# Reordering the hand-written schedule of a two-layer kernel: batch 2's projection between batch 0's pooled blocks, and four smaller moves

## The reference

```python
x = x + moe(lora(x, language_of_batch))          # layer 0
x = x + bit_ffn(attention_pool(x, kind_of_batch)) # layer 1
```

## Time and profile before

| | before |
|---|---|
| median of 3 runs | 734.63 us (733.26 to 735.54) |
| profiled execution: its time | 732.48 us |
| profiled execution: span from the first to the last instruction | 730.6 us |
| busy PE, DVE, ACT, POOL | 687.2, 474.9, 483.9, 390.2 us |

### The profile page before, as it was taken

How to read it: one execution, slowest core, us unless ns; L and a number is a source line. 1 busy time by engine, 2 the same in 40 slices (tenths; PEclk the granted TensorE clock), 3 DMA queues, 4 the chain that set the end, 5 groups by cost and what they waited for, 6 DMA issues and landing times.

```text
span 730.6 us, 9852 instructions
## 1 busy us (share of the span) xinstructions
PE 687.2 (94%) x3238; PEld 421.8 (58%) x3238; DVE 474.9 (65%) x866; ACT 483.9 (66%) x725; POOL 390.2 (53%) x427
## 2 busy tenths in 40 slices
PE   9899989999999999998788899999999999898997
PEld 6333667777777777783455455655556555453443
DVE  4288554545445545540356797887978879897895
ACT  1245436666367778871454979698796978968783
POOL 0202614563442615314867677777777767755554
PEclk9999999999999999999999999999999999999999
DMA  6999889998483948629302021131220111212122
GB/s 221 293 400 352 260 316 364 316 326 311 122 230 130 211 150 208 165 27 251 135 1 87 1 85 52 51 117 48 98 59 29 59 58 31 72 45 71 57 74 73
DMA packets 42627, 108.81 MB, mean 149 GB/s; under 512 B 5424, under 2 KB 7232, under 8 KB 39504
## 3 DMA queue, kind: packets, MB, share of 16 engines
q1 hardware_dynamic: 34352, 94.50, 36.7%
q0 software_dynamic: 7424, 13.06, 9.9%
q10 hardware_dynamic: 800, 0.61, 0.3%
HBM read 88.42 MB, written 28.13 MB: 160 GB/s over the span
## 4 chain that ended last, share of the span: by engine, by line
PE 48%; POOL 13%; issue 12%; ACT 7%; DVE 6%; DMA 3%; POOLq 0%; DVEq 0%; ACTq 0%; SPq 0%
PE ps L979 7%; PE ps L981 7%; PE ps L980 7%; PE ps L1416 6%; PE ps L1386 6%; PE ps L186 5%; POOL ht L1333 2%; POOL x_l L1237 2%; PE ps L971 2%; PE ps L970 2%; ACT h L1647 1%; ACT h L1640 1%; POOL xb L1341 1%; DMA choices<-token_choices,row_of_slot 1%; PE ps L1444 1%
## 5 line engine op out<-in xcount | busy, mean ns | idle before, releaser
L1386 PE MATMUL ps<-ff_q,qt 128*128 128x512 bf16 x512 | 124.2, 386 | 4.9 <-POOL qt L1295 3.3
L1416 PE MATMUL ps<-ff_q,ht 128*128 128x512 bf16 x512 | 120.8, 380 | 0.6 <-DVE res L1835 0.3
L797 POOL DMA_INDIRECT x_after_experts<-y,row_of_slot x32 | 51.6, 1612 | 130.0 <-DVE y L918 100.3
L979 PE MATMUL ps<-w_h,inner_l 128*128 128x512 f32 x256 | 102.0, 398 | 5.4 <-DVE inner_l L930 5.4
L1822 DVE SCALAR_TENSOR_TENSOR h<-ps,scale,bias 128x1024 f32<-128x1024 f32 x64 | 81.9, 1279 | 28.3 <-PE ps L1386 26.0
L981 PE MATMUL ps<-w_h,inner_h 128*128 128x512 f32 x256 | 100.1, 391 | 0.0
L980 PE MATMUL ps<-w_l,inner_h 128*128 128x512 f32 x256 | 100.0, 390 | 0.0
L865 ACT ACTIVATE inner_h<-ps 128x512 fp32r<-128x512 f32 x64 | 37.9, 592 | 70.5 <-PE ps L971 70.4
L1386 PEld LDWEIGHTS ps<-ff_q,qt 128*128 128x128 bf16 x512 | 48.0, 99 | 63.4 <-issue 8.2
L1827 DVE TENSOR_REDUCE h_mx<-h 128x1 f32<-128x1024 f32 x64 | 77.4, 1210 | 10.4 <-ACT h L1640 10.2
L1416 PEld LDWEIGHTS ps<-ff_q,ht 128*128 128x128 bf16 x512 | 48.8, 98 | 54.7 <-issue 1.8
(11 more groups left out here) (262 smaller groups left out, 1342.3 us busy)
## 6 DMA issues: line engine op xcount, KB each, us to landing
w_in_sb<-in_w_in_t SPq DMA_DIRECT2D x8, 2048.0 KB, 15.6
w_raw<-in_w_out_t SPq DMA_DIRECT2D x16, 1024.0 KB, 7.1
x_after_experts<-in_x SPq DMA_DIRECT2D x8, 1024.0 KB, 12.9
x_sum<-in_ff_t SPq DMA_DIRECT2D x8, 1024.0 KB, 9.8
raw<-in_ff_t SPq DMA_DIRECT2D x8, 1024.0 KB, 7.3
x<-x_after_experts SPq DMA_DIRECT2D x32, 256.0 KB, 2.9
out<-res SPq DMA_DIRECT2D x32, 256.0 KB, 3.1
x_sum<-x_after_experts SPq DMA_DIRECT2D x7, 1024.0 KB, 5.5
```

What stands on the lines that cost most here:

```text
L979: pe.matmul(ps[:, s, :], inner_l[:, r, c], w_h[:, k % RING, :], start=k == 0, stop=False)
L1386: m = pe.matmul(ps[:, ff_bank(t, half) + n, :], qt[:, t // TPB % 2, t % TPB, k, :], ff1_q[:, k, f * 512:(f + 1) * 512], start=k == 0, stop ...
L1416: mm = pe.matmul(ps[:, out_bank(t), :], ht[:, t % 2, k // 2, k % 2, :], ff2_q[:, k, :], start=k == 0, stop=k == KF - 1)
```

## The change

The edits, by block:

- Opening: `warm_up` counts 8, 2, 4 become 10, 4, 0. `expand(1, 1)` comes whole before `find(1, 0)`, where its last two products came after `find(1, 1)`.
- Last expert: `inner_block(e, 7)` comes ahead of `out_part(e, 5, 0)`, and the parts of s = 0 ahead of others.
- POOL: batch 1's two `x_low` come after `prob_low(0)` and after `exp_args(1)`; `x_high(2)` after `prob_low(1)`; `exp_args(2)` ahead of batch 2's `x_low`.
- PE: batch 2's `project` and `turn_x` lie between batch 0's pooled blocks; `turn_q(0)` ahead of `pool_block(1, 0)`. Other banks take batch 1's sums and batch 2's keys, and waits move with them.
- ACT: batch 0's squares in two pairs around `keep_x(2, 2..3)`, after `exps(1)`; `keep_sums(1)` before `attend(2)`.
- DVE: `norms(0)` before `greatest(0)`; `keep_q(0)` before `maxima(2)`.
- Loop, steps 22 and 26 (not full): `quantise` in two pieces, `turn_q` a step later, DVE's `keep_q` later.

```diff
-                    warm_up(pe, 8, FIND_BANK)
+                    warm_up(pe, 10, FIND_BANK)
...
-                    warm_up(pe, 2, FIND_BANK)
+                    warm_up(pe, 4, FIND_BANK)
...
-                    warm_up(pe, 4, FIND_BANK)
...
-                    expand(1, 1, range(0, 2))
+                    expand(1, 1)
                     find(1, 0)
                     find(1, 1)
-                    expand(1, 1, range(2, KD))
...
+                        inner_block(e, 7)
                         pe.wait_ge(in_l, KI * e + 6)
                         pe.wait_ge(w_l_cp, KI * e + 6)
                         out_part(e, 5, 0)
                         out_part(e, 5, 1)
-                        inner_block(e, 7)
-                        out_part(e, 5, 2)
                         pe.wait_ge(in_l, KI * e + 7)
                         pe.wait_ge(w_l_cp, KI * e + 7)
                         out_part(e, 6, 0)
-                        out_part(e, 6, 1)
                         pe.wait_ge(in_l, KI * e + 8)
                         pe.wait_ge(w_l_cp, KI * e + 8)
                         out_part(e, 7, 0)
+                        out_part(e, 6, 1)
                         out_part(e, 7, 1)
-                        out_part(e, 6, 2)
-                        out_part(e, 7, 2)
-                        for k in (5, 6, 7):
-                            out_part(e, k, 3)
+                        for s in (2, 3):
+                            for k in (5, 6, 7):
+                                out_part(e, k, s)
...
-            key_bank = lambda b: 0 if b == 1 else SMALL
+            key_bank = lambda b: {1: 0, 2: TRA}.get(b, SMALL)
...
-            num_bank = lambda b, j: (NUM, 0, 1, OUT)[j] if b < 2 else (NUM, NUM, ATT_BANK, NUM)[j]
+            num_bank = lambda b, j: ((NUM, 0, 1, OUT), (0, 1, NUM, OUT))[b][j] if b < 2 else (NUM, NUM, ATT_BANK, NUM)[j]
...
-                    for b in (0, 1):
-                        x_high(b)
-                        x_low(b, 0)
-                        x_low(b, 1)
+                    x_high(0)
+                    x_low(0, 0)
+                    x_low(0, 1)
+                    x_high(1)
...
                     exp_args(0)
                     split_side_keys(0)
                     prob_low(0)
+                    x_low(1, 0)
                     exp_args(1)
-                    x_high(2)
+                    x_low(1, 1)
                     split_side_keys(1)
                     gains(0)
                     prob_low(1)
+                    x_high(2)
+                    unpack_q(0)
+                    exp_args(2)
                     x_low(2, 0)
-                    unpack_q(0)
                     x_low(2, 1)
-                    exp_args(2)
...
-                            pe.wait_ge(pool_cp, 2 * TPB - 1)
+                            pe.wait_ge(pool_cp, TPB + 2)
...
+                        if b == 3 and k == 1:
+                            pe.wait_ge(key_cp, 3)
...
-                        elif b >= 2:
+                        elif b >= 3:
                             pe.wait_ge(sum_l_cp, 2 * b)
...
-                        if j == (1 if b >= 2 else 0) and b + 1 < BATCH:
+                        if j == 1 and b != 1 and b + 1 < BATCH:
                             pe.wait_ge(key_cp, b + 2)
...
-                    for j in range(TPB):
-                        pool_block(0, j)
+                    pool_block(0, 0)
+                    pool_block(0, 1)
                     project(2, 0)
                     project(2, 1)
                     turn_x(2, 2, -1)
                     turn_x(2, 3, -1)
+                    pool_block(0, 2)
+                    pool_block(0, 3)
+                    side_sums(1)
                     project(2, 2)
                     project(2, 3)
-                    side_sums(1)
                     score(2)
-                    pool_block(1, 0)
                     turn_q(0)
-                    for j in range(1, TPB):
+                    for j in range(TPB):
                         pool_block(1, j)
...
-                        if j == 2 and inside(bq, BATCH):
+                        if j == 2 and inside(bq, BATCH) and full(i):
                             turn_q(bq)
                         if j == 3 and inside(bp, BATCH):
                             pool_block(bp, 2)
+                        if j == 3 and inside(bq, BATCH) and not full(i):
+                            turn_q(bq)
...
-                    for j in range(TPB):
-                        square(0, j)
                     exps(1)
+                    square(0, 0)
+                    square(0, 1)
                     keep_x(2, 2)
                     keep_x(2, 3)
+                    square(0, 2)
+                    square(0, 3)
                     prob_high(1)
+                    keep_sums(1)
                     attend(2)
-                    keep_sums(1)
...
                         if inside(t0, TILES):
                             gelu_half(t0, 0)
+                        if j == 2 and inside(bq, BATCH) and not full(i):
+                            quantise(bq, range(0, 2))
...
+                        if j == 2 and inside(bq, BATCH) and not full(i):
+                            quantise(bq, range(2, TPB))
...
+                    norms(0)
                     greatest(0)
-                    norms(0)
                     sums_low(1)
                     keep_keys(2)
+                    keep_q(0)
                     maxima(2)
-                    keep_pool(1, 0)
-                    keep_q(0)
-                    for j in range(1, TPB - 1):
+                    for j in range(TPB - 1):
                         keep_pool(1, j)
...
-                            if j == 3 and inside(bq, BATCH):
-                                keep_q(bq)
                             if inside(t3 - 1, TILES) and not full(i - 1):
                                 finish(t3 - 1)
                             if inside(t0, TILES):
                                 add_bias(t0, 0)
                             if inside(t2, TILES):
                                 keep_h(t2)
+                            if j == 3 and inside(bq, BATCH):
+                                keep_q(bq)
```

More of the change, by code:

```diff
@@ L1616, in attend, with quantise @@
                         act.activation(att[:], ps[:, att_bank(b), :], ACT.Tanh, bias=att_b_sb[:, 0:1]).then_inc(att_done, 1)
-                    def quantise(b):
+                    def quantise(b, js=range(TPB)):
                         act.wait_ge(to_q1_ready, b + 1)
@@ L1621, in quantise @@
                             act.wait_ge(q_tr, b)
-                        for j in range(TPB):
+                        for j in js:
                             act.activation(q8[:, j, :], pool_sb[:, j, :], ACT.Copy, scale=to_q1[:, j:j + 1]).then_inc(q8_ready, 1)
```

## The result

| | before | after |
|---|---|---|
| median of 20 runs | 735.52 us (732.30 to 738.53) | 732.62 us (728.02 to 736.85) |
| profiled execution: time, span | 732.48, 730.6 us | 728.02, 726.2 us |

The ratio is 0.9941, 95% interval 0.9924 to 0.9958: 4.3 us faster (3.1 to 5.6). I had predicted 11.6 us faster and a time of 723.0, range 718.5 to 730.5. The sign is right, the size is not, and the time lies outside the range. Of the gap of 9.6 in time, 0.9 is the base: the median that I started from, of three runs, was 734.63, that of twenty is 735.52. (The two medians lie only 2.9 apart, the means of the twenty runs 3.8; I go by the ratio, so 7.3 of the forecast 11.6 are missing.) After's profiled execution was the fastest of its twenty.

What follows compares the result with a forecast made beforehand. PE was taken as the bound, busy 687.2 of 730.6 us. Terms -1.7 - 1.4 - 6.0 - 2.5 = -11.6 took the profiled 732.48 to 720.9; with the median 2.15 above, 723.0 us, range 718.5 to 730.5.

Steps and rivals of the forecast that it cites:

- Last expert, -1.4: Last expert: y of s = 0 ready 1.39 us early, the fourth scatter and the load of x following; -1.4 us.
- a bound of 0: Last expert's bound: no gain if the scatters are delayed by the mask's load, which lies beside them.
- Attention, -6.0: Attention of batches 0 to 2: exp_args(0) no longer waits behind batch 1's x_low, turn_q(1) at 409.6, not 415.55; -6.0 us.
- My lower bound of -3: Attention of batches 0 to 2: only -3 us if one more cover fails.
- Last steps, -2.5: Steps 22 and 26: +0.95 us at step 24 and -3.45 at step 28; sum -2.5 us.
- Opening, -1.7: Opening: the barrier opens 2.07 us early and expert 0's choices land earlier; -1.7 us, bounds -0.8 and -2.5.
- rival (3): Opening: without a warm-up right ahead of feats the clock comes up only after several batches; 737.4 us, chance 0.06.
- rival (1): Opening and one attention piece give little: choices land with the loads, keep_q(0) holds up maxima(2); 730.0 us, chance 0.18.
- rival (4): The edits cancel, attention gains reappearing as idle PE before qt of batch 1; within 2 us of 734.6, chance 0.07.
- (2): Attention: the clock falls in the new gap before turn_q(0) and at tile 2; 727.8 us, chance 0.14.
- the 1.63 in the prediction: Attention: the time in us that DVE's top took beside POOL's x_low, against 0.69 in the seven other batches.
- the stricter rule: Attention: two-input VectorE and GpSimd operations on SBUF exclude each other; a late x_low(1, 0) would leave -3.6, not -5.1.

Runs made afterwards that it cites:

- f3: The changed kernel with ACT's rounding of block 6 moved behind w_h and inner_h of the last expert's last block: 732.06 us, 0.9930 of the kernel before.
- g1: The changed kernel with the attention mask's load issued behind the loads of x: 722.65 us, 0.9861 of the kernel before.
- g2: The changed kernel with the mask's load behind the loads of x and ACT's rounding late in the last expert: 724.60 us, 0.9863 of the kernel before.
- h3: The changed kernel with the old order of the last expert and the mask's load behind the loads of x: 727.96 us, 0.9898 of the kernel before.
- h4: The changed kernel with two warm-ups back ahead of feats, ACT's rounding late and the mask's load late: 728.52 us, 0.9902 of the kernel before.
- e3: The kernel before with only the attention edits of batches 0 to 2: 731.08 us, 0.9933 of the kernel before.
- f2: The kernel before with SP's copies of x for batches 2 to 4 held until expert 0's slot weights are known: 748.82 us, 1.0161 of the kernel before.
- e1: The kernel before with only the opening's edits: 735.51 us, 0.9985 of the kernel before.
- e2: The kernel before with only the last expert's new order: 736.44 us, 1.0019 of the kernel before.
- e4: The kernel before with only the edits of steps 22 and 26: 735.44 us, 0.9984 of the kernel before.
- f4: The changed kernel with the old order of the last expert: 732.84 us, 0.9921 of the kernel before.
- h2: The changed kernel with two warm-ups put back ahead of feats: 730.67 us, 0.9937 of the kernel before.
- f1: The changed kernel with SP's copies of x for batches 2 to 4 held until expert 0's slot weights are known: 740.71 us, 1.0024 of the kernel before.

## Why the prediction was wrong, step by step

**Last expert, -1.4: the step that failed outright; it is +1.1.** I costed PE's parts (right: f3 has y 1.37 early) and put at nothing, without a reason, the wait for the low part of block 7. ACT's 1.5 us of rounding stands ahead of `w_h(7)`, and PE now arrives before it is through: 0.67 of waiting, shown by f3. "The load lies beside them" was named as a bound of 0; it is a loss. With the old order the mask's load goes out 1.5 us before the fourth scatter, which lands after 5.8 to 6.5; with the new one 0.15 before, which lands after 7.2 to 8.2; with the mask late after 5.7 to 6.0, whichever the order. Shown by g1, g2, h3 and h4. That is 2.5 of the missing microseconds.

**Attention, -6.0: the path is as I said, but I read its gain from one state of the clock; it is 2.1 to 5.4.** In e3, less the 4.2 by which x lands later than in the earlier trace rows, `turn_q(0)` comes at 380.6 (predicted 380.25), the first `first_matrix` at 386.9 (386.05), `turn_q(1)` at 410.2 (409.6), step 4 at 425.1: 7.0 early where I said 6.0, as the product of 3.38 in the earlier trace rows takes 1.89. That product is the first thing that other executions lack: of the five traces of the old order only before has it, for 1.5 us of its 90.15.

The second is larger. In the old order POOL makes `x_low(1)` ahead of `exp_args(0)`, and that hides a slow start. `exp_args(0)` begins 15.2 or 15.3 us after x landed in before and f2, whose clock held there, and 15.6 in e1, e2 and e4, whose clock was low there and whose first score came 1.6 to 1.7 us later. Moreover, in these three PE waits 1.9 to 2.0 before `side_sums(0)`, not the 3.26 of the earlier trace rows, and the products behind it are not slow (e1, timelines of POOL, DVE and PE; x landed at 344.94):

```profile
355.11 4.67 POOL L1235 TENSOR_TENSOR x_l<-x_sum,x_h 128x1024 fp32r<-128x1024 f32 x2
358.06 2.26 DVE L1788 TENSOR_TENSOR top<-run_max 128x512 f32 x1 [0.16 <-DVE run_max L1785]
360.50 1.16 POOL L1271 TENSOR_TENSOR prob<-mask,top 128x512 f32<-128x512 f32 x1 [0.73 <-DVE top L1788]
364.44 0.43 PE L1465 MATMUL ps<-x_l,side_key_r 128*48 128x512 f32 x1 [1.91 <-POOL side_key_r L1221]
```

So the old order loses nothing by a low clock where x lands; it needs 87.2 with it and 88.5 (f2) without. The new order has taken that cover away and pays in full: `exp_args(0)` begins 12.3 us after x where the clock held and 13.9 to 14.0 where it was low, and **b** is 83.1 to 83.4 (e3, f3, f4, h3) against 84.9 to 85.1 (eight traces, after's 85.12 among them). Like with like, the new order wins 5.1 to 5.4 us where the clock holds as x lands and 2.1 to 2.3 where it doesn't. The mean over the traces that leave the mask's load alone is 3.0 us, or 3.5 with before among the old ones; e3's runs say 4.9, give or take 1.8. This step accounts for 0.6 to 3.9 of the missing microseconds, by the state of the clock, and 2.5 to 3.0 by the means. My lower bound of -3 spoke of covers that fail, not of a loss that the old order covers and the new one doesn't.

**Last steps, -2.5: mis-sized, -1.7.** The DVE wait before `keep_q(6)` was to be about 2 (1.93); step 24, against step 4, is 1.03 late (predicted 0.95); the wait before `turn_q(7)` was to be 1.6 (1.58) and step 28 is 2.3 early against step 4. Then 0.5 comes back at the end, where PE waits 1.06 for ACT's `narrow_h` in place of 0.52: I had followed the gain no further than step 28.

**Opening, -1.7: not refuted, -1.1 with an interval that holds 0, and by other terms than mine; if the size is right, it is partly luck.** The barrier was to open 2.07 early. The old opening turns expert 0's rows at 75.6 to 76.6 (five traces), the new one at 71.1 to 71.9 in four traces and at 73.7 to 76.7 in eleven (the mean of the fifteen is 74.1, 2.0 before that of the five; h2 and h4, one in each group, have two warm-ups back): two populations, told apart by the clock in the first two `feats`: 7.06 us for sixteen records in the four, 8.8 to 9.9 in the others, 7.7 to 8.9 with the old warm-ups. That is the mechanism of my rival (3), but at most seven records of the first batch's eight are slow, not four batches. What is won there meets ACT's stop where it occurs: `inner_h` of blocks 3 and 4 starts up to 10 us after PE's product, PE idles 3.4 to 8.1 us (0 to 3.7 without the stop, for the choices), and its next products can run at half the clock (those from 97 to 100 in after lie 0.43 apart, not 0.23). From the turn to M are 230.7 to 234.9 us without the stop and 235.7 to 239.7 with it (f1 and f2 left out). Among the traces with the stop M still comes 2.2 earlier in the mean with the new opening (eight traces against three). In the earlier trace rows there is no stop, so the prediction's path (choices, `w_slot`, `inner_l`) was read from the case that most sittings did not show. Why ACT stops isn't settled: full DMA queues are ruled out (f1, f2), POOL's gathers and a place in ACT's instructions were tried only where nothing stopped.

**Rivals.** The change of 4.3 us is nearest to rival (1), which has 4.6, though not for its reasons; the time of 732.62 lies as near to the edge of rival (4), 732.6. Landing between them is the sum of one step with the wrong sign, one that depends on the clock and two that are slightly small, and says nothing for either. (2) and (3) both exist, as outcomes of single executions rather than of the kernel. (4)'s mechanism did not happen: what the attention won stayed won at step 4.

## What to carry to other kernels

Before summing gains from one profile, ask how much of the stretch that you shorten is idle or low clock that another execution would not have; a second profile of the same code, or one of a harmless variant, shows it, and here it was worth up to 4 of 11.6 us. Ask also which losses the old order hides: an order that shortens the path makes every delay ahead of it count. When an order is changed on the bounding engine, check the engine that feeds its last block and the transfer that is issued beside its result: PE's parts came 1.4 early, and ACT's rounding and an unrelated load took 2.5 back. A load nobody waits for yet belongs behind those on the path: moving the mask's was one line, won 1.9 us of the stretch in which it lay, and the medians of the four kernels that have it are 1.6 to 4.1 us below those of the same sitting that don't. And compare a variant with its own sitting piece by piece: part of such a difference can lie where the edit does nothing.

## What the runs showed of the hardware

A DVE operation that reads two tiles of SBUF (`top`, `side_max`) did not get through beside a POOL operation that reads SBUF (`x_low`): it ended only when that was over. In all five traces of the old order `top` was issued while an `x_low` ran and ended 0.54 to 0.55 us after its end, so it took 1.60 to 2.33 us; in before and f2 the small `side_max`, 0.16 elsewhere, then took 2.3, until the second `x_low` ended. In the fifteen traces of the new order, where `x_low(1, 0)` is over 0.24 us or more before it, `top` took 0.69 every time. So the 1.63 in the prediction was no constant price, and the stricter rule that it sets beside it is the one that these rows bear out. DVE's running maxima, which read PSUM, took 1.22 beside an `x_low`, as without one.

An indirect scatter of a quarter of an expert's rows, the fourth of the last expert, lands 5.7 to 6.5 us after its issue, and 7.2 to 8.2 when a bulk load was issued 0.15 us ahead of it. Where x lands, PE's wait and the clock behind it went together: with waits of 0.25 to 1.45 us the clock held in four traces of four, with 1.54 to 2.66 it fell in eleven of sixteen, for 1.7 us of loss; the same code in the same place does either. The Trainium skill (TensorE: Matmul & The Clock Gate, "PE-mode transpose") says that transposes don't count as work for the clock; the wait before `turn_q(0)` is followed by transposes in all fifteen traces of the new order, and the clock fell there in one, whose wait was 1.47 us and not 0.53 or 0.54; that neither bears out the rule nor refutes it. And an engine can stand still for 4 to 11 us with its inputs ready and the DMA queues at a share of 0.19, in some sittings and not in others.
